# Two of four first loads moved to another queue, and three warm-up products dropped: a fused attention and spiking-MLP block

## What is computed

```python
xn = layernorm(x)
q, k, v = split(xn @ w_qkv)              # 16 heads of 16
mask = sigmoid(mask_logits)              # 9 frequencies
q = irfft(rfft(q) * mask); k = irfft(rfft(k) * mask)
attn = softmax(q @ k.T / 4) @ v
a = attn @ w_out + b_out
h = square(relu(xn @ W_fc.T)); y = h @ W_proj.T
for _ in range(5):                       # leaky integrate and fire
    mem = 0.9 * mem + y - (mem > 1); spikes += mem > 1
out = x + a + spikes / 5
```

## Time and profile before

| | us |
|---|---|
| median of the runs (1691.52 to 1691.74) | 1691.6 |
| the profiled execution | 1691.07 |
| its span, first to last instruction | 1689.3 |
| TensorE busy | 1681.4 |
| VectorE busy | 1494.2 |
| ScalarE busy | 1330.1 |
| GpSimd busy | 719.7 |

### The profile page before, as it was taken

The page is one execution under the profiler, slowest core; times in us unless marked ns, Lnnn a source line. Parts: engine busy times, 40 slices in busy tenths (PEclk is TensorE's granted clock), DMA queues, the critical chain, the costliest instruction groups (busy, mean ns, idle before and its releaser), DMA issues.

```text
span 1689.3 us, 44435 instructions
## 1 busy us (share of the span) xinstructions
PE 1681.4 (100%) x17842; PEld 1145.9 (68%) x17842; DVE 1494.2 (88%) x2375; ACT 1330.1 (79%) x1718; POOL 719.7 (43%) x979
## 2 busy tenths in 40 slices
PE   9999999999999999999999999999999999999999
PEld 6566666666666666666666666666666666666667
DVE  6889999998999999989998999999989998999884
ACT  5548888888888888888888888888888888888872
POOL 3103334555433345554333455543335554333455
PEclk9999999999999999999999999999999999999999
DMA  6851122112211221122112211221122112211133
GB/s 216 294 161 47 33 54 55 51 33 55 55 50 34 55 55 43 41 55 55 43 41 55 56 37 47 55 55 36 48 55 56 31 53 55 55 30 54 43 105 103
DMA packets 95406, 108.02 MB, mean 64 GB/s; under 512 B 56032, under 2 KB 70240, under 8 KB 95200
## 3 DMA queue, kind: packets, MB, share of 16 engines
q1 hardware_dynamic: 91744, 101.97, 21.2%
q10 hardware_dynamic: 3456, 3.21, 0.6%
HBM read 78.91 MB, written 20.97 MB: 59 GB/s over the span
## 4 chain that ended last, share of the span: by engine, by line
PE 98%; DVE 1%; ACT 0%; issue 0%; ACTq 0%; POOL 0%; POOLq 0%
PE banks L735 31%; PE ring L711 22%; PE ring L718 14%; PE ring L724 14%; PE banks L841 7%; PE banks L846 3%; PE banks L659 2%; PE ring L928 2%; PE ring L672 1%; PE ring L645 1%; PE ring L659 1%; PE ring L686 0%; DVE stats L947 0%; DVE attnT L979 0%; ACT xnT L513 0%
## 5 line engine op out<-in xcount | busy, mean ns | idle before, releaser
L562 ACT ACTIVATE probs<-ring 128x1024 f32<-128x1024 f32 x1024 | 1002.1, 1026 | 6.5 <-PE ring L724 6.2
L711 PE MATMUL ring<-kst,qst 64*128 64x512 f32 x2000 | 674.7, 417 | 0.3 <-ACT probs L562 0.3
L735 PE MATMUL banks<-probs,vst 128*32 128x256 f32 x8192 | 548.2, 385 | 0.1
L1036 DVE TENSOR_REDUCE pmax<-ring 128x2 f32<-128x1024 f32 x407 | 497.7, 1223 | 12.7 <-PE ring L711 0.5
L568 ACT ACTIVATE half_sb<-ring 128x512 f32<-128x512 f32 x500 | 299.2, 598 | 261.4 <-PE ring L711 254.1
L718 PE MATMUL ring<-qst,kst 64*128 64x512 f32 x2048 | 493.0, 425 | 0.1
L711 PEld LDWEIGHTS ring<-kst,qst 64*128 64x128 f32 x2000 | 328.3, 184 | 208.3 <-issue 204.6
L1017 DVE TENSOR_REDUCE pmax<-ring 128x1 f32<-128x512 f32 x500 | 345.4, 691 | 88.7 <-PE ring L711 85.1
L724 PE MATMUL ring<-shift_rows,ones 64*128 64x512 f32 x2048 | 422.9, 390 | 0.0
L1023 DVE TENSOR_REDUCE pmax<-half_sb 128x1 f32<-128x512 f32 x500 | 335.5, 671 | 37.0 <-ACT half_sb L568 33.1
L735 PEld LDWEIGHTS banks<-probs,vst 128*32 128x32 f32 x8192 | 213.7, 109 | 209.7 <-issue 91.0
(11 more groups left out here) (96 smaller groups left out, 1050.9 us busy)
## 6 DMA issues: line engine op xcount, KB each, us to landing
kst<-qk_scratch SPq DMA_DIRECT2D x256, 128.0 KB, 3.0
qst<-qk_scratch SPq DMA_DIRECT2D x256, 128.0 KB, 2.9
qk_scratch<-attnT SPq DMA_DIRECT2D x32, 256.0 KB, 3.0
shift_rows<-shiftT SPq DMA_DIRECT2D x512, 2.0 KB
qk_scratch<-probs SPq DMA_DIRECT2D x16, 256.0 KB, 3.0
attnT<-o_turned SPq DMA_DIRECT2D x256, 16.0 KB, 1.9
xnT<-x SPq DMA_DIRECT2D x8, 512.0 KB, 5.6
out<-xnT SPq DMA_DIRECT2D x7, 512.0 KB, 2.9
```

The lines of the kernel that those rows point to most:

```text
L562: act.activation(probs[:, s % PS, :], score_slot(g), ACT.Exp, scale=SCALE).then_inc(exp_done, 1)
L711: return pe.matmul(unit_slot(g)[:, c * BLK:(c + 1) * BLK], qst[b][rows, tile * P:(tile + 1) * P], kst[b][rows, key:key + BLK], start=True, ...
L735: mm = pe.matmul(po[32 * j:32 * (j + 1), half * D:(half + 1) * D], vst[b][:, kt, :], quarters[:, j], start=(kt == 0), stop=(kt == TB - 1))
L1036: dve.tensor_reduce(pmax[:, tile, 2 * part:2 * part + 2], unit_slot(g).rearrange("p (c e) -> p c e", c=2), AX, ALU.max).then_inc(mx_taken, 1)
```

## The change

The third and fourth tile of block 0 are no longer issued by SyncE. ScalarE issues them, ahead of its loads of the logits and of the DFT matrix. SyncE's loads of `ident`, `wqk`, `wv` and block 1 keep their order and follow two issues earlier. The warm-up of TensorE has seven products in place of ten. Nothing else is touched, and the waits are the same.

```diff
-WARM = 10
+WARM = 7
...
         @block.sync
         def _(sp):
-            for k in range(KT):
+            for k in range(KT // 2):
                 sp.dma_start(x_in[:, 0, k, :], x_blocks[0][:, k, :]).then_inc(first_x[k], 16)
             sp.dma_start(ident[:], eye).then_inc(ident_in, 16)
             sp.dma_start(wqk_raw, wqk).then_inc(wqk_in, 16)
...
         @block.scalar
         def _(act):
 
+            for k in range(KT // 2, KT):
+                act.dma_start(x_in[:, 0, k, :], x_blocks[0][:, k, :]).then_inc(first_x[k], 16)
             act.dma_start(filt[:, 0:1], logits).then_inc(logits_in, 16)
             act.dma_start(dft_sb, dft).then_inc(dft_in, 16)
             act.wait_ge(logits_in, 16)
```

## The result

The changed kernel is slower: 1693.78 us in the median of 22 runs (1692.06 to 1695.04), where the kernel before has 1691.12 in 22 runs (1690.7 to 1691.82). The ratio is 1.0016, with a 95% interval of 1.001 to 1.0022. That is 2.7 us, where 1.0 us less had been forecast. The profiled execution took 1693.84 us, with a span of 1692.0 against 1689.3. Two executions further down, one of the kernel before (2721.18 us) and one of `e6_dft_on_sync` (3227.61 us), were slow ones and count in no ratio.

The account below looks back on a forecast made before the run. TensorE was taken to bound the kernel, its start set by its own queue (ready 8.61) and the normalisation (8.93). Transposes at 8.93 instead of 9.89 gain 0.96 us: 1691.6 - 0.96 = 1690.6 us, range 1690.0 to 1691.8.

Parts of the forecast that it names:

- What bounds the start: First block: transposes wait for TensorE's queue, ready at 8.61, and the scaled block, at 8.93; they start 0.96 us earlier.
- TensorE's share of the gain: Warm-up: three fewer products save TensorE 1.28 us; alone, stopped by the scaling's end at 9.30, they gain about 0.54 us.
- The tiles: Block 0's third and fourth tile on ScalarE's queue: fourth lands by 4.48, statistics end about 5.1, 0.7 us earlier.
- The logits: ScalarE's load issued at 1.64 lands after 2.7 to 3.3 us; Sqrt at 6.23, normalisation 0.42 us earlier.
- the far end: Start of block 0: logits take 4.6 us, Sqrt at 7.8, reciprocal at 8.1, kernel 0.6 us slower, 1692.2 us.
- The DFT matrix: ScalarE's load issued at 2.1 lands at 4.8 to 5.4, before the gate's last step needs it at about 6.0.
- Rival (A): First block's loads: shared DMA engines or late logits eat the normalisation's gain; 1691.0 to 1691.3 us as a rule; chance 0.18.
- Rival (B): Folding at 7.62: the clock rises after the warm-up has ended, kernel slower, 1691.9 to 1693.5 us; chance 0.11.
- Rival (C): After the start: a later fixed wait takes the gain before the end; time 1691.6 us; chance 0.05.
- Chances and range: Whole kernel: forecast 0.65, "same" within 0.2% 0.97, slower 0.02, faster 0.01; range 1690.0 to 1691.8 us.
- The rule on issuing engines: Loads at the start: issuers share 16 DMA engines, so the fourth tile gains at most its 0.92 us of issue.

Follow-up runs that it names:

- e6_dft_on_sync: Changed kernel, but ScalarE issues logits before the two tiles and SyncE the DFT matrix before `ident` and `wqk`; 1691.43 us against 1692.41 for the kernel before.
- e5_hold_wqk: Changed kernel, but SyncE waits for the DFT matrix to land before issuing `wqk`, `wv` and block 1; one run, 1692.45 us against 1692.41 for the kernel before.
- e4_logits_first: Changed kernel, but ScalarE issues only the logits ahead of the two tiles, the DFT matrix behind them; 1693.66 us against 1691.70 for the kernel before.
- e2_warm7_only: Kernel before with seven warm-up products in place of ten, all loads untouched; 1691.40 us against 1691.70, ratio 0.9999.
- e7_warm12: Changed kernel with twelve warm-up products in place of seven; 1693.49 us against 1692.41 for the kernel before, ratio 1.0007.
- e1_tiles_only: Changed kernel with ten warm-up products kept, so only the two tiles move; 1693.69 us against 1691.70 for the kernel before, ratio 1.0011.

## Why the prediction was wrong, point by point

- **What bounds the start.** Right in its form: two chains meet at the transposes, TensorE's own queue and the normalisation. TensorE's share of the gain was real: seven products alone moved the transposes from 9.89 to 9.45, where 9.35 was forecast.
- **The tiles.** Right: the statistics ended at 5.05, forecast 5.1, with the fourth tile in time.
- **The logits: the step that failed.** I bounded their landing by 2.7 and 3.3 us, rows of a trace in which the second queue carried nothing but two small loads and `wqk` stood behind all four tiles. It was 5.5 (4.7 to 5.6 in other executions with the same order of loads), beyond even the 4.6 of the far end. The Sqrt came at 8.65 instead of 6.23. I had counted that `wqk` goes out 0.93 us earlier, and counted it only as a gain; what it does beside the small loads I put at nothing. With the large loads held back (`e5_hold_wqk`) the logits took 3.2 us and the reciprocal came at 6.58, inside my bounds, so the chain behind the logits was right.
- **The DFT matrix.** The same error, and as large: 2.7 to 3.3 forecast, 6.3 measured. I called it covered, but it stands on VectorE ahead of the reciprocal, and with the logits in time it still costs 2.0 us (`e4_logits_first`).
- **Rival (A)** named the shared engines and the late logits, and had them at most 0.6 us slower, with a chance of 0.18. The mechanism was right and the term mis-sized: normalisation 1.97 us late (the scaling starts at 9.89 for 7.92), where its far end had 1.2.
- **Rival (B)** named the clock. Its place and trigger were off. The rise did come later than in the execution that I read, at about 7.2 us, but seven products at the slow pace also last longer, until 7.38 and not 7.03, and the rise still fell inside them. The clock was up and then fell, at 10.6 us in the folding here, and at about 8.5 in the gap in another execution. With the loads in time it fell in none of eleven runs (`e2_warm7_only`). I treated (A) and (B) as excluding each other, but (A) made the gap behind which the clock fell. The length of the gap alone does not decide it: it fell behind 1.48 us and held through 2.56 (`e4_logits_first`). Their sum is the result: by the medians about 1.9 us for late loads and 1.5 for the clock on one chip, 3.5 together.
- **Rival (C)** is out: the shift at 16 us is still there at 114 us and at the end.
- **Chances and range.** "Within 0.2%" holds, 0.16% slower. The range ended at 1691.8, and the median is 2.0 us beyond it. The range left out what happens when two rivals come together. The 0.3 us that I allowed for two medians was also too small: the kernel before itself measured 1691.12, 1691.70, 1692.41 and 1691.72 on its four occasions after the forecast.
- **The rule on issuing engines** that the prediction took from the Trainium skill ("DMA: Bandwidth & Descriptors", "Issuing engines are not separate DMA queues") bounded the gain: the statistics ended 0.77 us earlier, under the 0.92 of issue. As I used it, it did not speak of what the loads behind would lose, and I did not ask.

Two sizes stay open. Of the 1.9 us that the version with fourteen products loses, 1.50 is the later start of the transposes (11.39 for 9.89). And the tiles alone lose 2.0 us in the median where their profiled execution has a span only 1.2 longer: eight of the eleven runs have a mean clock of 1.000 and still lie between 1692.3 and 1694.1. The traces show where such differences arise. From ScalarE's exponential at 163 us to the one at 1588 us, all of it work that no edit touches, it is 1424.5 us before and with the tiles alone, 1424.8 in the changed kernel, 1425.2 with fourteen products, 1425.5 in `e6_dft_on_sync` and 1425.7 in `e7_warm12`. The gain of 1.1 us that `e6_dft_on_sync` has at 163 us is 0.1 at 1588, against the one trace of the kernel before. So up to 1.2 us come and go over the whole kernel. Why is not shown, nor is what the chip and what the execution have in it. A single trace therefore prices only the start, and differences under about 1 us need the medians of one chip.

## What to carry to other kernels

A load moved to a second queue also changes what runs beside the loads left behind: list every load on both queues with its row size, and expect a load of small rows to land late beside one of large rows. Put small loads that gate a chain ahead of the first large one; in `e6_dft_on_sync` they landed after 2.6 and 2.8 us. A warm-up should last until the first real product is released, and when that release moves, its length has to be set again.

## What the runs showed of the hardware

- Two queues that both had work moved nearly equal counts of packets and not equal bytes: 37 packets of 4 KB beside 40 of 1 KB in the same microsecond, with the engines filled to 58%. The load of 512 bytes took 2.5 to 2.7 us issued first on its queue, 3.2 behind two tiles, 4.0 with 1 KB rows and then 4 KB rows beside it, and 4.7 to 5.6 with the 4 KB rows first.
- The clock's first rise does not stand at a fixed time. The fourteen records of seven products took 5.23 us in one execution and 6.30 in another, so the slow pace of 0.43 us lasted until about 5.0 and 7.2 us; the twenty of ten products took 7.23 and 6.06, so until about 6.5 and 4.1 (from the lengths, with 0.21 us for each fast start):

```profile
1.08 6.06 PE L688 MATMUL ring<-lif 128*128 128x256 f32 x20 [1.08 <-POOL lif L411]
```

- The Trainium skill, "TensorE: Matmul & The Clock Gate", "What you observe", gives the rise a spread of half a microsecond either way from run to run; the four executions here spread over 3 us, and the measurement decides.
- The granted clock reads 1.00 while the first products run at half pace (the earlier trace rows beside the earlier trace rows); only falls after the first rise showed in that column.
- A gap on TensorE does not bring the clock down by its length alone: behind one of 1.48 us it fell in one execution of the change, at 10.6 us and with TensorE at work again, and during one of 3.02 it fell in another, while it held through 1.17 (`e1_tiles_only`) and 2.56 us (`e4_logits_first`).
